# First stage of a two-layer perceiver kernel: transforms in both sets of PSUM banks, root and scaling on ScalarE ahead of the weight splits, biases added by VectorE

## The reference, cut to what matters

```python
x = x + _L0_xattn_ref(_layernorm(x), ctx_1024, ctx_1024, Wq, bq, Wk, bk, Wv, bv, Wo, bo)

q = (queries @ Wq + bq).reshape(B, Lq, H, DK)
k = (keys @ Wk + bk).reshape(B, Lk, H, DK)[:, :Lq]
v = (values @ Wv + bv).reshape(B, Lk, H, DK)[:, :Lq]
qf, kf = rfft(q over tokens), rfft(k over tokens)
c = qf.real * kf.real + 1j * -(qf.imag * kf.imag)
mean_value = jnp.mean(irfft(c, n=Lq), axis=(heads, dims))     # 32 numbers a sequence
weights, delay = jax.lax.top_k(mean_value, 6)
# v is shifted by the six delays, summed with softmax(weights), and goes through Wo and bo
```

## Time and profile before

| | us |
|---|---|
| median of three runs | 2225.07 |
| the profiled execution, its own time | 2229.75 |
| its span (first to last instruction) | 2227.7 |
| first matmul of the first unit `qf` 0 | 41.7 |
| first matmul of the first value unit `av` 0 | 95.2 |
| mean granted TensorE clock | 0.976 |

### The profile page before, as it was taken

How to read it: one execution, slowest core, us unless ns; L and a number is a source line. 1 busy time by engine, 2 the same in 40 slices (tenths; PEclk the granted TensorE clock), 3 DMA queues, 4 the chain that set the end, 5 groups by cost and what they waited for, 6 DMA issues and landing times. The chain is left out here.

```text
span 2227.7 us, 35893 instructions
## 1 busy us (share of the span) xinstructions
PE 2104.9 (94%) x14950; PEld 1526.9 (69%) x14950; DVE 1259.3 (57%) x2098; ACT 916.9 (41%) x2207; POOL 72.6 (3%) x111
## 2 busy tenths in 40 slices
PE   6999898799999999989999999999999999989999
PEld 5773454478867877734446788778878778775587
DVE  4356289363336788899999210544344454456663
ACT  3234334153424333599996432332232232333442
POOL 0000000000000000100000000000000000000122
PEclk9999898799999999999999999999999999999999
DMA  6020000112110111020003144321121121232001
GB/s 241 20 103 1 1 1 3 40 57 76 38 44 20 57 38 57 20 95 19 1 1 114 58 132 151 100 68 62 44 87 44 44 87 44 68 115 93 1 1 38
DMA packets 84872, 127.01 MB, mean 57 GB/s; under 512 B 6998, under 2 KB 48470, under 8 KB 84248
## 3 DMA queue, kind: packets, MB, share of 16 engines
q1 hardware_dynamic: 84712, 124.73, 16.9%
HBM read 109.77 MB, written 14.94 MB: 56 GB/s over the span
## 5 line engine op out<-in xcount | busy, mean ns | idle before, releaser
L1228 ACT ACTIVATE R<-bank 128x512 f32<-128x512 f32 (+3 forms) x157 | 93.0, 597 | 459.2 <-PE bank L909 332.2
L1473 ACT ACTIVATE R<-R 128x64 f32<-128x64 f32 x1024 | 248.5, 370 | 0.0
L909 PE MATMUL bank<-cth,wmh 128*128 128x512 f32 x512 | 207.9, 406 | 8.5 <-ACT arena L1574 7.3
L909 PE MATMUL bank<-cth,wml 128*128 128x512 f32 x512 | 202.2, 395 | 0.0
L909 PE MATMUL bank<-ctl,wmh 128*128 128x512 f32 x512 | 201.9, 394 | 0.0
L508 PE MATMUL bank<-XN,arena 128*128 128x512 f32 x320 | 150.5, 623 | 0.0
L909 PEld LDWEIGHTS bank<-cth,wmh 128*128 128x128 f32 x512 | 96.1, 188 | 37.7 <-issue 16.7
L508 PE MATMUL bank<-Y,arena 128*128 128x512 f32 x256 | 117.1, 603 | 0.0
L2233 DVE COPY Y<-bank 128x512 f32<-128x512 f32 x128 | 79.5, 682 | 60.8 <-PE bank L947 60.8
L508 PEld LDWEIGHTS bank<-XN,arena 128*128 128x128 f32 x320 | 62.3, 201 | 74.0 <-issue 73.4
L909 PEld LDWEIGHTS bank<-cth,wml 128*128 128x128 f32 x512 | 96.2, 188 | 22.2
(11 more groups left out here) (417 smaller groups left out, 4414.5 us busy)
## 6 DMA issues: line engine op xcount, KB each, us to landing
H<-in_ctxT SPq DMA_DIRECT2D x30, 512.0 KB, 5.1
arena<-in_L_attn_mlp_w SPq DMA_DIRECT2D x8, 1024.0 KB, 5.2
arena<-spill SPq DMA_DIRECT2D x32, 256.0 KB, 5.5
spill<-R SPq DMA_DIRECT2D x3, 2048.0 KB, 8.3
spill<-XN SPq DMA_DIRECT2D x3, 2048.0 KB, 8.3
arena<-in_L_ffn_Wg SPq DMA_DIRECT2D x4, 1024.0 KB, 7.5
arena<-in_L_ffn_Wu SPq DMA_DIRECT2D x4, 1024.0 KB, 5.2
arena<-in_L_ffn_Wd SPq DMA_DIRECT2D x4, 1024.0 KB, 5.4
```

What stands on the lines that cost most here:

```text
L909: last = mm(b[:, :].rearrange("p (a c) -> p a c", a=2), w_, c_[:, k, :, :], start=(k == 0 and n_ == 0), stop=(k == 3 and n_ == 2))
L1228: fn(dst, src, ACT.Copy).then_inc(act_bank_free, 1)
L1473: last = fn(EE[n % 3][:, a:a + 64], RC["Ey"][:, t, h, :], ACT.Copy, scale=RC["Ex"][:, t, h, 8 * j + x:8 * j + x + 1])
```

## The change

Eight transforms alternate between the rings, even tiles in ring A and odd ones in ring V, for both context and stream. The root's table is loaded by an activation ahead of the context's high parts. VectorE splits two context tiles before the statistics, one between them and the reciprocal, the other five after the scaling. It scales the even stream tiles; ScalarE scales the odd ones with a factor and an offset (minus mean times factor, made by a new small VectorE operation). The weight split of Wk comes directly behind the first `ldq` low part. The bias matmuls, the split biases and `dc_r` are gone: the biases are loaded as 128 equal rows, and VectorE adds them, times 32 in the rows of frequency zero, while it reads `qf` and `kf` out of their banks; the product then reads two SBUF tiles. ScalarE no longer copies `qf`.

```diff
 # TensorE
+            def transformed(name, rows_, t):
+                b = open_dve((name, t)) if t % 2 else open_act((name, t))
+                for k in range(4):
+                    last = mm(b[:, tl(k)], rows_[:, t, tl(k)], tab("dft"), start=True, stop=True)
+                last.then_inc(dve_bank_full if t % 2 else act_bank_full, 1)
             for t in range(TT):
+                transformed("ldk", ctm, t)
             for t in range(TT):
-                pe.wait_ge(xn_tile, t + 1)
+                pe.wait_ge(S["a_xn"] if t % 2 else xn_tile, t // 2 + 1)
+                transformed("ldq", xtm, t)
-            pe.wait_ge(S["a_blo"], 1)
-            on_act(("ldk", TT - 1))
             for t in range(TT):
-                on_dve(("ldq", t))
+                if t % 2:
+                    on_dve(("ldq", t))
+                else:
+                    on_act(("ldq", t))
...
                     pe.wait_ge(S["a_wlo"], i + 1)
                     b = open_dve((name, t)) if i else open_act((name, t))
-                    mm(b[:, :], dc_r[:, :], bias_parts[:, i, :], start=True, stop=False)
 # ScalarE
-            fn(dc_r[:, :], tab("dc", 33), ACT.Copy)
+            warm()
             for t in range(TT):
-                b = unit(("ldk", t))
+                b = transformed("ldk", t)
                 fn(lk_high[:, :, tl(t)], ..., ACT.Copy).then_inc(S["a_khi"], 1)
             act.wait_ge(a_var, 1)
             fn(small[:, 0:8], RA["mv"][:, :, 1], ACT.Sqrt, bias=tab("eps")).then_inc(a_std, 1)
-            act.wait_ge(in_small, 32)
-            fn(bias_parts[:, :, :], bias_raw, ACT.Copy).then_inc(S["a_bhi"], 1)
+            act.wait_ge(S["a_nm"], 1)
+            for t in range(1, TT, 2):
+                fn(xtm[:, t, :], xtm[:, t, :], ACT.Identity, scale=small[:, t:t + 1], bias=small[:, 8 + t:9 + t]).then_inc(S["a_xn"], 1)
             first_weight_high(0)
...
-                copy_out(RA["qs"][:, t % 2, :], b[:, :])
+                act.wait_ge(act_bank_full, UA.at[("qf", t)] + 1)
 # VectorE
+            for t in range(2):
+                key_low(t)
             dve.wait_ge(in_xtm, 16)
...
+            key_low(2)
             dve.wait_ge(a_std, 1)
             step(v.reciprocal(small[:, 0:8], small[:, 0:8]))
-            for t in range(TT):
+            v.scalar_tensor_tensor(small[:, 8:16], RA["mv"][:, :, 0], -1.0, small[:, 0:8], ALU.mult, ALU.mult).then_inc(S["a_nm"], 1)
+            for t in range(0, TT, 2):
                 v.tensor_scalar(xtm[:, t, :], ...).then_inc(xn_tile, 1)
-            dve.wait_ge(S["a_bhi"], 1)
-            v.tensor_tensor(bias_parts[32:33], ...).then_inc(S["a_blo"], 1)
+            for t in range(3, TT):
+                key_low(t)
             first_weight_low(0)
+            query_low(0)
+            first_weight_low(1)
+            for t in range(1, TT):
+                query_low(t)
+            dve.wait_ge(in_small, 32)
             for t in range(TT):
+                u, qs = UA.at[("qf", t)], RA["qs"][:, t % 2, :]
+                dve.wait_ge(act_bank_full, u + 1)
+                v.scalar_tensor_tensor(qs, RA["bias"][:, 0, :], tab("dc"), UA.banks[u % 4][:, :], ALU.mult, ALU.add).then_inc(act_bank_free, 1)
+                v.scalar_tensor_tensor(first_keys, RA["bias"][:, 1, :], tab("dc"), unit(("kf", t))[:, :], ALU.mult, ALU.add).then_inc(dve_bank_free, 1)
                 on_act(("qf", t))
-                v.tensor_tensor_reduce(out=RA["qs"][:, t % 2, :], in0=RA["qs"][:, t % 2, :], in1=b[:, :], ...).then_inc(dve_bank_free, 1)
+                stored(("kf", t))
+                step(v.tensor_tensor_reduce(out=qs, in0=qs, in1=first_keys, ...))
 # SP
-                sp.dma_start(bias_raw[:, i, :], dram["first_bias"][:, i, :]).then_inc(in_small, 16)
+                sp.dma_start(RA["bias"][:, i, :], dram["first_bias"][i:i + 1, :].to_broadcast([128, D])).then_inc(in_small, 16)
```

More of the change, by code:

```diff
@@ L60, in constant_tables @@
     tabs["rank"] = np.tile(np.arange(8.0) - 8.0, (128, 1))
[L61 to L64, removed]
+    tabs["dc"] = np.where(p[:, None] % 32 == 0, 32.0, 0.0)
     ex = np.zeros((128, 512))
@@ L558, in _ @@
                     b = open_dve((name, t)) if i else open_act((name, t))
-                    mm(b[:, :], dc_r[:, :], bias_parts[:, i, :], start=True, stop=False)
                     three(b[:, :], (lambda k: high[:, k, tl(t)], lambda k: first_high_of(i)[:, k, :]),
-                          (lambda k: low[:, k, tl(t)], lambda k: first_low[:, i, k, :]), first=False
+                          (lambda k: low[:, k, tl(t)], lambda k: first_low[:, i, k, :])
                           ).then_inc(dve_bank_full if i else act_bank_full, 1)
@@ L1274, in _, with transformed @@
             act.wait_ge(in_consts, 32)
-            fn(dc_r[:, :], tab("dc", 33), ACT.Copy)
+            def transformed(name, t):
+                if t % 2:
+                    u = UV.at[(name, t)]
+                    act.wait_ge(dve_bank_full, u + 1)
+                    return UV.banks[u % 4]
+                return unit((name, t))
+            warm()
             for t in range(TT):
-                b = unit(("ldk", t))
+                b = transformed("ldk", t)
                 fn(lk_high[:, :, tl(t)], b[:, :].rearrange("p (k n) -> p k n", k=4), ACT.Copy).then_inc(S["a_khi"], 1)
@@ L1280, in _ @@
             fn(small[:, 0:8], RA["mv"][:, :, 1], ACT.Sqrt, bias=tab("eps")).then_inc(a_std, 1)
-            act.wait_ge(in_small, 32)
-            fn(bias_parts[:, :, :], bias_raw, ACT.Copy).then_inc(S["a_bhi"], 1)
+            act.wait_ge(S["a_nm"], 1)
+            for t in range(1, TT, 2):
+                fn(xtm[:, t, :], xtm[:, t, :], ACT.Identity, scale=small[:, t:t + 1], bias=small[:, 8 + t:9 + t]).then_inc(S["a_xn"], 1)
             first_weight_high(0)
             for t in range(TT):
-                act.wait_ge(dve_bank_full, UV.at[("ldq", t)] + 1)
-                b = UV.banks[UV.at[("ldq", t)] % 4]
+                b = transformed("ldq", t)
                 fn(lq_high[:, :, tl(t)], b[:, :].rearrange("p (k n) -> p k n", k=4), ACT.Copy).then_inc(S["a_qhi"], 1)
@@ L1299, in _ @@
                     first_weight_high(t - 1)
+            act.wait_ge(act_bank_free, UA.at[("qf", TT - 1)] + 1)
             copy_out(VA[:, 0, :], unit(("av", 0))[:, :])
@@ L1799, in first_weight_low, with transformed, key_low, query_low @@
                                 ).then_inc(S["a_wlo"], 1)
-            for t in range(TT):
+            def transformed(name, t):
+                return UV.banks[UV.at[(name, t)] % 4] if t % 2 else UA.banks[UA.at[(name, t)] % 4]
+            def key_low(t):
                 dve.wait_ge(S["a_khi"], t + 1)
-                b = UA.banks[UA.at[("ldk", t)] % 4]
-                v.tensor_tensor(lk_low[:, :, tl(t)], b[:, :].rearrange("p (k n) -> p k n", k=4), lk_high[:, :, tl(t)].bitcast(f32),
-                                ALU.subtract).then_inc(act_bank_free, 1)
+                v.tensor_tensor(lk_low[:, :, tl(t)], transformed("ldk", t)[:, :].rearrange("p (k n) -> p k n", k=4),
+                                lk_high[:, :, tl(t)].bitcast(f32), ALU.subtract).then_inc(dve_bank_free if t % 2 else act_bank_free, 1)
+            def query_low(t):
+                dve.wait_ge(S["a_qhi"], t + 1)
+                v.tensor_tensor(lq_low[:, :, tl(t)], transformed("ldq", t)[:, :].rearrange("p (k n) -> p k n", k=4),
+                                lq_high[:, :, tl(t)].bitcast(f32), ALU.subtract).then_inc(dve_bank_free if t % 2 else act_bank_free, 1)
+            for t in range(2):
+                key_low(t)
             dve.wait_ge(in_xtm, 16)
@@ L1819, in _ @@
-            v.tensor_tensor(bias_parts[32:33], bias_raw[32:33], bias_parts[32:33].bitcast(f32), ALU.subtract).then_inc(S["a_blo"], 1)
+            for t in range(3, TT):
+                key_low(t)
             first_weight_low(0)
-            for t in range(TT):
[L1822 to L1827, removed]
@@ L1828, in _ @@
-            for t in range(TT):
+            query_low(0)
[3 more added lines that the diff above has]
+            dve.wait_ge(in_small, 32)
+            for t in range(TT):
+                u, qs = UA.at[("qf", t)], RA["qs"][:, t % 2, :]
+                dve.wait_ge(act_bank_full, u + 1)
+                v.scalar_tensor_tensor(qs, RA["bias"][:, 0, :], tab("dc"), UA.banks[u % 4][:, :], ALU.mult, ALU.add
+                                       ).then_inc(act_bank_free, 1)
+                v.scalar_tensor_tensor(first_keys, RA["bias"][:, 1, :], tab("dc"), unit(("kf", t))[:, :], ALU.mult, ALU.add
+                                       ).then_inc(dve_bank_free, 1)
@@ L1829, in _ @@
                 on_act(("qf", t))
-                b = unit(("kf", t))
-                v.tensor_tensor_reduce(out=RA["qs"][:, t % 2, :], in0=RA["qs"][:, t % 2, :], in1=b[:, :], scale=1.0, scalar=0.0,
-                                       op0=ALU.mult, op1=ALU.add, accum_out=RA["C"][:, 0, t:t + 1]).then_inc(dve_bank_free, 1)
+                stored(("kf", t))
```

(12 more changed lines are left out.)

9 lines of the change are left out of this document (2 added, 7 removed).

## The result

The changed kernel takes 2206.65 us (median, 2205.82 to 2207.73) beside 2225.53 for the kernel before: 18.9 us less, ratio 0.9915 with the 95% interval 0.9897 to 0.9932. The forecast was 2205.3, 19.8 less, in a range of 2202.5 to 2211.

The account below looks back on a forecast made before the run. TensorE's work was taken to bound the units and VectorE's one queue the head before them. Head 9.8 plus units 10.0 gave 19.8 us less, from the median 2225.07 to 2205.3 us, range 2202.5 to 2211.

Parts of the forecast that it names:

- Units: Sixteen units from `qf` 0 to `av` 0: 3.34 to 2.72 us each without the 33-row matmul, 10.0 us less.
- the bounds (16 x 0.35 stay or go): Units: at most 10.0 us less; 5.6 us stay if the 0.35 gap belongs to the unit's start.
- Statistics' start: Head, VectorE: with only two low parts ahead, the statistics begin at 16.15 instead of about 22.5.
- VectorE's queue: Head, after the statistics: scalings end at 24.65, five context low parts 27.95, Wq's low part 30.15, `query_low(0)` 30.8.
- The clock: TensorE stands 2.1 us before the stream's transforms; a fall to half clock costs 0 to 1.9, taken as 1.0.
- The first unit: End of the head: `qf` 0 starts at 31.9, between 30.9 (data-bound) and 32.8, instead of 41.7.
- 9.8 us less: The head's term: `qf` 0 at 31.9 against 41.7.
- everything waits in its one queue: Before the units VectorE is the chain: low parts, statistics, scaling, splits.
- The cover for what was moved: Moved work stays hidden: `cx` 1.85 after `av` 0, which covers 2.7; ScalarE's scalings 2.8, weight-split slack 0.4.
- Rivals (b) to (d): Late head, 2209.3, chance 0.08; units at half clock, 2244.9, 0.03; VectorE bounds the units, 2208.3, 0.04.

Follow-up runs that it names:

- the second one of before: The kernel before, unchanged, traced a second time: 2229.45 us for the traced run, span 2227.4, `av` 0 at 94.4.
- the two runs with one more matmul: Changed kernel, each of the sixteen units starting with one extra, overwritten matmul, over 33 rows or over 128: 2216.23 and 2208.25 us.
- the head alone: Changed kernel with the bias matmuls, split biases, copies of `qf` and large table put back: 2218.26 us, ratio 0.9958 to the kernel before.
- the root's table late: Changed kernel without the activation ahead of the context's high parts, so the root's table loads where the root stands: 2211.49 us.
- the last version: Changed kernel with the stream tokens sent ahead of the tables that are wanted late: 2207.02 us, ratio 0.9923 to the kernel before.

## Why the prediction was right, step by step

- **The forecast** (19.8 us) holds: 18.9 in the medians, whose interval reaches from 15.1 to 22.9; 21.8 between the spans of the two first traces, 21.0 up to `av` 0 against the second one of before. The mechanism is right; that the medians lie within 0.9 of the forecast is partly luck. In the traces the head gained 2.2 more than its term, and the scatter between runs gave that back.
- **Units**, predicted 10.0, were 53.48 - 43.69 = 9.8. The choice between the bounds (16 x 0.35 stay or go) was right, and the two runs with one more matmul show why.
- **Statistics' start**: predicted 16.15, was 15.52. They followed the second low part, as forecast, and that began 0.5 earlier (14.91, not 15.41), since TensorE started at 10.46 and not 10.96. The rest is a reading of mine: I counted from the end of the low part, while the row of the statistics starts 0.61 after that of the low part in both traces (21.88 and 22.49 before). The tokens had landed by 2.11 + 13.2 = 15.3.
- **VectorE's queue** from there to the start of Wq's low part: predicted 11.8, was 11.2. The five low parts took 0.61 each and not 0.66, and the root began at 21.06, right behind the aggregation, and not at 21.9, as ScalarE's last high part was done by 20.5.
- **The clock**: I put 1.0 between 0 and 1.9. It held in this trace (2.52 us of standing, where I had counted 2.1) and in those with 2.41, 2.75 and 2.83; it fell in those with 2.95, 3.12 and 3.19, for 1.6, 1.6 and 2.6 us up to the first unit. The upper end, transforms done 2.3 later (32.8 against 30.5), was too low by 0.3, and 1.0 is what neither branch gives.
- **The first unit**: predicted 31.9 within 30.9 to 32.8, was 29.75, outside these bounds by 1.1. That is the three points above: 0.6 at the statistics, 0.6 in the queue, 1.0 for the clock. The data were there at 29.60, and the transforms ended just behind them. The term "9.8 us less" was 12.0 against the first trace and 11.2 against the second. Against the medians this error is hidden by their scatter.
- **What bounded it**: "everything waits in its one queue" was half the truth. In the kernel before the waits for banks held up the first unit by 2.3 to 3.1 us, which I had taken up only as a condition (no transform short of a bank) and not as a term. The total did not suffer, since I worked out the start of `qf` 0 in the changed kernel from both sides.
- **The cover for what was moved** held. `cx` started 1.82 after `av` 0 (75.26), forecast 1.85, and TensorE did not wait for it. The delay weights were ready at 89.6, the last value copy at 96.4. ScalarE's scalings took 2.93 for four, forecast 2.8, and the weights were split in time, but narrowly: the high part of Wk was done at 29.44 and VectorE took it at 29.52, a slack of 0.1 us where I had counted 0.4.
- Rivals (b) to (d) left no trace: Wq's and Wk's high parts were made in time for VectorE, which did not wait for them; VectorE waited for TensorE in every tile of the units from the second on; the units ran at 1.00.

## What to carry to other kernels

A matmul of another form among equal ones can cost more than its columns, as the one over 33 rows did here (0.61 us for 0.22 of columns): count the gaps of the weight loads on either side of it, and see whether another engine that reads the result anyway can take over its work. Where an engine's queue decides, ask of each operation in it who waits for it: work that nobody wants yet, ahead of the one that starts the next stage, was worth 7.9 us here without a single instruction saved, 1.9 of them because TensorE's clock did not fall. A ring of four banks can bound a stretch in which the engine that frees them looks like the chain; work out the start of the next stage from the data and from the banks.

## What the runs showed of the hardware

The granted clock can fall after TensorE has taken up work again: in the trace of the head alone it stood for 3.12 us, worked for 1.4 us at 1.00 and then went to 0.50 for over 3 us. With the root's table late it stood for 3.19 us, nearly as long, and the clock fell 1 us before the work began; the cost up to the first unit was 1.6 us in the one and 2.6 in the other. So the cost of a stand of about 3 us is not settled by the stand's length alone.

At the start of the program the first two or three transforms come up to 1.70 us apart and the later ones 0.89, though the granted clock reads 1.00 for all of them. How many are slow differs from trace to trace, and the eight take 8.84 to 10.26 us.

Behind `av` 0, with the same work of TensorE, the twelve traces lie between 2127.9 and 2133.8 us. The time at half the clock there differs as well, by the granted clock roughly from 86 to 100 us, without setting the order of the spans alone. What else is in it stays open; no run was made for it. With a few runs a kernel a difference of 1 us, like that of the last version, is seen in the trace only.
